# Interaction and deep network of a recommendation model: two accumulator banks used in turn, spreads in groups of three, and a new order of gathers and dumps

## What is computed

```python
emb = tables[feat_idx, sparse]                       # 2048 x 26 x 32
linear_out = lin_sparse_w[feat_idx, sparse].sum(-1) + dense @ lin_dense_w
x0 = emb; xk = emb; res = []
for w, bb in ((conv1_w, conv1_b), (conv2_w, conv2_b)):
    hp = jnp.einsum('bhd,bmd->bhmd', xk, x0).reshape(-1, h * M, E)
    xn = sigmoid(jnp.einsum('oi,bid->bod', w, hp) + bb[None, :, None])
    xk = xn[:, :half]; res.append(xn[:, half:])
cin_out = (concat(res).sum(-1) @ cin_w + cin_b)[:, 0]
h1 = tanh(deep_x @ W1 + b1); h2 = tanh(h1 @ W2 + b2); h3 = tanh(h2 @ W3 + b3)
return linear_out + cin_out + (h3 @ deep_w + deep_b)[:, 0] + bias[0]
```

## Time and profile before

| | us |
|---|---|
| median of 3 executions | 1631.12 (1628.97 to 1633.01) |
| the profiled execution, whole | 1624.22 |
| its span, first to last instruction | 1622.4 |
| PE busy | 1543.6 (95%) |
| DVE busy | 1104.7 (68%) |
| POOL busy | 709.2 (44%) |
| ACT busy | 643.5 (40%) |

### The profile page before, as it was taken

One profiled execution on the slowest core, in us unless ns is written; L12 is line 12 of the kernel. 1 busy time (PEld: TensorE's weight loads), 2 busy tenths in 40 slices (PEclk: granted clock), 3 DMA queues, 4 the chain that ended last, 5 costly groups with the idle time before them and its releaser, 6 DMA issues.

```text
span 1622.4 us, 23599 instructions
## 1 busy us (share of the span) xinstructions
PE 1543.6 (95%) x6584; PEld 656.8 (40%) x6584; DVE 1104.7 (68%) x1017; ACT 643.5 (40%) x904; POOL 709.2 (44%) x600
## 2 busy tenths in 40 slices
PE   0598999999999999999999999999999999999999
PEld 0232333333333333333333333333333336787876
DVE  3276777777777877787777777787877783333332
ACT  2342434344434443434443434434343323344443
POOL 7356565556555556565555646464731110000000
PEclk9899999999999999999999999999999999999999
DMA  6688999999999999999998989898999884634531
GB/s 126 143 183 194 231 214 223 217 231 209 226 212 225 211 224 209 221 214 229 210 228 200 232 201 231 201 240 201 237 203 235 204 210 122 186 120 147 175 104 53
DMA packets 178599, 319.80 MB, mean 197 GB/s; under 512 B 31132, under 2 KB 106812, under 8 KB 178524
## 3 DMA queue, kind: packets, MB, share of 16 engines
q1 hardware_dynamic: 155423, 298.87, 75.0%
q10 hardware_dynamic: 9828, 13.43, 4.1%
q0 software_dynamic: 13312, 7.06, 3.8%
HBM read 297.93 MB, written 21.31 MB: 197 GB/s over the span
## 4 chain that ended last, share of the span: by engine, by line
PE 86%; issue 4%; DVE 3%; another core or an unknown queue 2%; POOL 2%; DMA 1%; SPq 1%; ACT 1%; ACTq 0%; DVEq 0%; POOLq 0%
PE y L751 42%; PE xn L745 19%; PE bc L880 16%; PE bc L731 5%; PE bc L738 3%; DVE hp L692 2%; POOL emb L542 2%; PE bc L723 1%; DVE xb L692 1%; SPq L465 1%; DMA x0t<-x_halves 1%; DMA x_lo<-dense_halves 0%; ACTq L370 0%; DMA emb<-table,idx_stage 0%
## 5 line engine op out<-in xcount | busy, mean ns | idle before, releaser
L692 DVE TENSOR_TENSOR hp<-bc,xk 128x1024 f32<-128x1024 f32 x384 | 453.9, 1219 | 271.3 <-PE bc L731 136.0
L542 POOL DMA_INDIRECT emb<-table,idx_stage x416 | 515.9, 1240 | 145.5 <-issue 126.3
L692 DVE TENSOR_TENSOR xb<-xb,xk 128x1024 f32<-128x1024 f32 x448 | 546.5, 1264 | 27.9 <-ACT xk L927 23.9
L751 PE MATMUL y<-xb,w2s 128*64 128x512 f32 x1792 | 436.0, 601 | 0.0
L745 PE MATMUL xn<-sq,w1s 128*128 128x512 f32 x768 | 369.7, 618 | 4.4 <-issue 4.4
L751 PE MATMUL y<-hp,w2s 128*64 128x512 f32 x1536 | 366.0, 597 | 0.0
L553 POOL TENSOR_TENSOR r<-r 128x512 f32<-128x512 f32 x96 | 123.5, 1287 | 351.0 <-ACT r L932 181.3
L926 ACT ACTIVATE xk<-xn,bias 64x512 f32<-64x512 f32 x128 | 87.4, 683 | 438.5 <-PE xn L745 248.8
L922 ACT ACTIVATE sq<-bc 128x1024 f32<-128x1024 f32 x192 | 182.9, 1026 | 197.5 <-PE bc L738 145.8
L751 PEld LDWEIGHTS y<-xb,w2s 128*64 128x64 f32 x1792 | 116.0, 136 | 248.8 <-issue 201.5
L745 PEld LDWEIGHTS xn<-sq,w1s 128*128 128x128 f32 x768 | 137.5, 192 | 162.6 <-issue 154.8
(11 more groups left out here) (57 smaller groups left out, 843.3 us busy)
## 6 DMA issues: line engine op xcount, KB each, us to landing
xb<-x_rows SPq DMA_DIRECT2D x896, 256.0 KB
w_raw<-W SPq DMA_DIRECT2D x32, 448.0 KB
x0t<-x_halves ACTq DMA_DIRECT2D x252, 52.0 KB
x_halves<-deep_halves SPq DMA_DIRECT2D x30, 384.0 KB
w_raw<-W SPq DMA_DIRECT2D x16, 512.0 KB
emb<-table,idx_stage POOLq DMA_INDIRECT x416
x_hi<-x_halves SPq DMA_DIRECT2D x24, 256.0 KB
x_lo<-x_halves SPq DMA_DIRECT2D x24, 256.0 KB
```

What stands on the lines that cost most here:

```text
L542: nc.gpsimd.indirect_dma_start(out=emb[:, m, :], out_offset=None, in_=table, in_offset=bass.IndirectOffsetOnAxis(ap=idx_stage[:, m:m + 1], ...
L692: nc.vector.tensor_tensor(product(n)[:, :], x[:, :], xk[sl % 2][:, :], ALU.mult).then_inc(multiplied, 1)
L751: last = nc.tensor.matmul(y2[H * c:H * c + H, :], w2s[:, ORDER[n], :], src[:, c * CHUNK:(c + 1) * CHUNK], start=(n == 0), stop=(n == PAIRS ...
```

## The change

- `acc[0]` and `acc[1]` take the place of `xn` and `y2`. In step sl the first layer's half c goes to `acc[(sl + c) % 2]`, the second layer to `acc[sl % 2]`. Half 0 still waits for the reads of the last step's halves; half 1 waits for `read_y2` of the step before, which used its bank; contraction 0 waits for the read of half 0. In the prologue half 1 waits for nothing.
- PE spreads the pairs n = 3, 4, 5, 8, 9, 10 in two groups of three, with row groups 0, 1, 0 and 1, 0, 1 (`ORDER`). The order on PE is now: K fills; contractions 8 to 10; D fills; contractions 11, 12; fills 3, 4, 5; first half 0; first half 1; fills 8, 9, 10; contractions 0 to 7. All slots of a group are waited for ahead of it. DMA spreads n = 0, 1, 2, 6, 7, 11, 12.
- The last step has an order of its own (`FINAL_WORK`), and the linear terms come after all its contractions but the last five.
- The turning of the next tile's rows is in step 1 for tile 0 too. `dump_halves` and `dump` are issued together at the end of step 1's spreads.
- POOL gathers the last seven fields of a tile ahead of the sum of `r2`, not around it. In tile 0 thirteen gathers are issued at once, and thirteen one by one, each after one product of step 0 (`multiplied`).
- The 16 loads of the deep network's first group are issued in four parts in the four steps of tile 15, not all in its last step.

Changed lines of the diff (context and blank lines are left out):

```diff
@@ -52,8 +52,8 @@
-ORDER = [0, 1, 2, 3, 8, 4, 5, 9, 6, 7, 10, 11, 12]
-BY_PE = (3, 4, 6, 7, 9, 10)
+ORDER = [0, 1, 2, 3, 8, 4, 5, 6, 9, 7, 10, 11, 12]
+BY_PE = (3, 4, 5, 8, 9, 10)
@@ -65,12 +65,18 @@
-    ("fill", (3, 4)),
+    ("fill", (3, 4, 5)),
+    ("first", 1),
+    ("fill", (8, 9, 10)),
+    ("of_this", (0, 1, 2, 3, 4, 5, 6, 7)),
+)
+FINAL_WORK = (
+    ("of_last", (8, 9, 10, 11, 12)),
+    ("fill", (3, 4, 5)),
-    ("fill", (6, 7)),
-    ("first", 1),
-    ("fill", (9, 10)),
+    ("fill", (8, 9, 10)),
@@ -81,9 +87,8 @@
-def deep_step(ahead):
-    return 2 if ahead == 3 else 1
+DEEP_STEP = 1
@@ -91,7 +96,7 @@
-    if ahead == 0 or sl != deep_step(ahead):
+    if ahead == 0 or sl != DEEP_STEP:
@@ -112,7 +117,7 @@
-assert all(group_of(BY_PE[i]) != group_of(BY_PE[i + 1]) for i in range(0, len(BY_PE), 2))
+assert all(group_of(n) != group_of(n + 1) for n in BY_PE if n + 1 in BY_PE)
@@ -239,8 +244,10 @@
-        xn = pb("xn", [P, CHUNK])
-        y2 = pb("y2", [P, CHUNK])
+        acc = [pb(f"acc{i}", [P, CHUNK]) for i in range(2)]
+        terms = acc[(STEPS - 2) % 2]
@@ -322,6 +329,9 @@
+        def first_acc(sl, c):
+            return acc[(sl + c) % 2]
@@ -333,7 +343,7 @@
-            tile(0, True, 3)
+            tile(0, True, 2)
@@ -478,15 +488,13 @@
-                        if i == 2 and sl == 2 and not is_first and ahead > 0:
-                            dump_halves(t + 1)
-                    if sl == 2 and is_first:
+                    if sl == DEEP_STEP and ahead > 0:
-                    if sl == deep_step(ahead) and ahead > 0:
-                    if sl == STEPS - 1 and ahead == 0:
-                        sp.wait_ge(dense_dumped, 64)
-                        load_x(0, 0, 1)
+                    if ahead == 0:
+                        if sl == 0:
+                            sp.wait_ge(dense_dumped, 64)
+                        load_x(0, sl, STEPS)
@@ -571,40 +579,33 @@
+                    for n in range(PAIRS):
+                        pool.wait_ge(multiplied, n + 1)
+                        hold()
+                        gather((PAIRS + n,), gathered)
-                        gather(range(AHEAD[2], AHEAD[2] + 3), gathered)
+                        gather(range(AHEAD[2], M), gathered)
-                    if ahead > 0:
-                        gather(range(AHEAD[2] + 3, M), gathered)
-                if is_first:
-                    gather(range(PAIRS, M), gathered)
-                elif ahead > 1:
-                    free_emb(t + 1, filled_by(t, 1, ("D", DEEP_N - 1), ahead))
+                if ahead > 1:
+                    free_emb(t + 1, filled_by(t, DEEP_STEP, ("D", DEEP_N - 1), ahead))
-                if is_first:
-                    add_up(t, 1, r2, r2_step, y2_read, 1, sum2)
-                    free_emb(t + 1, filled_by(t, 2, ("D", DEEP_N - 1), ahead))
-                    gather(range(9), gathered)
-                else:
-                    if ahead > 1:
-                        gather(range(AHEAD[0], AHEAD[0] + 3), gathered)
-                    add_up(t, 1, r2, r2_step, y2_read, 1, sum2)
-                    if ahead > 1:
-                        gather(range(AHEAD[0] + 3, AHEAD[1]), gathered)
+                if ahead > 1:
+                    gather(range(AHEAD[0], AHEAD[0] + 3), gathered)
+                add_up(t, 1, r2, r2_step, y2_read, 1, sum2)
+                if ahead > 1:
+                    gather(range(AHEAD[0] + 3, AHEAD[1]), gathered)
-                if is_first:
-                    gather(range(9, 13), gathered)
-                elif ahead > 1:
+                if ahead > 1:
-                if is_first:
-                    gather(range(13, AHEAD[2]), gathered)
-                elif ahead > 1:
+                if ahead > 1:
@@ -690,10 +691,10 @@
-                        if n == 3 and sl == deep_step(ahead) and ahead > 0:
+                        if n == 3 and sl == DEEP_STEP and ahead > 0:
-                        if n == 5 and sl == deep_step(ahead) and ahead > 0:
+                        if n == 5 and sl == DEEP_STEP and ahead > 0:
@@ -739,16 +740,16 @@
-            def contract_k(c):
+            def contract_k(c, acc_k):
-                    last = nc.tensor.matmul(xn[:, :], w1s[:, k, :], sq[k][:, cols], start=(k == 0), stop=(k == K1 - 1))
+                    last = nc.tensor.matmul(acc_k[:, :], w1s[:, k, :], sq[k][:, cols], start=(k == 0), stop=(k == K1 - 1))
-            def contract(n):
+            def contract(n, acc_y):
-                    last = nc.tensor.matmul(y2[H * c:H * c + H, :], w2s[:, ORDER[n], :], src[:, c * CHUNK:(c + 1) * CHUNK],
+                    last = nc.tensor.matmul(acc_y[H * c:H * c + H, :], w2s[:, ORDER[n], :], src[:, c * CHUNK:(c + 1) * CHUNK],
@@ -792,15 +793,14 @@
-            contract_k(0)
-            pe.wait_ge(xn_read, 1)
-            contract_k(1)
+            for c in range(2):
+                contract_k(c, first_acc(-1, c))
-                    last = nc.tensor.matmul(xn[32 * g:32 * g + 1, 0:CHUNK], w, x[:, g * CHUNK:(g + 1) * CHUNK],
+                    last = nc.tensor.matmul(terms[32 * g:32 * g + 1, 0:CHUNK], w, x[:, g * CHUNK:(g + 1) * CHUNK],
@@ -808,7 +808,7 @@
-                        nc.tensor.matmul(xn[32 * g:32 * g + 1, c * P:(c + 1) * P], lin_sum[:, t:t + 1], idf[:, :],
+                        nc.tensor.matmul(terms[32 * g:32 * g + 1, c * P:(c + 1) * P], lin_sum[:, t:t + 1], idf[:, :],
@@ -817,44 +817,46 @@
-                    for kind, what in STEP_WORK:
+                    for kind, what in FINAL_WORK if final else STEP_WORK:
-                                if is_product(use):
+                                if not is_d(use):
-                                if not is_product(use):
+                                if is_d(use):
-                                contract(n)
-                            if final and what[-1] == PAIRS - 1:
-                                pe.wait_ge(xn_read, ALL_STEPS * 2)
-                                pe.wait_ge(end_loaded, END_LOADED)
-                                pe.wait_ge(lin_done, TILES)
-                                add_term(cwd[:, :], dense_rows, start=True)
-                                add_linear()
+                                contract(n, acc[(sl - 1) % 2])
-                            if what[0] == 0 and not start:
-                                pe.wait_ge(y2_read, s)
+                            if what[0] == 0:
+                                pe.wait_ge(xn_read, s * 2 + (2 if final else 3))
-                                contract(n)
+                                contract(n, acc[sl % 2])
-                            pe.wait_ge(xn_read, s * 2 + (2 + what))
-                            contract_k(what)
+                            if what == 0:
+                                pe.wait_ge(xn_read, s * 2 + 2)
+                            elif not start:
+                                pe.wait_ge(y2_read, s)
+                            contract_k(what, first_acc(sl, what))
+                        pe.wait_ge(y2_read, s)
+                        pe.wait_ge(end_loaded, END_LOADED)
+                        pe.wait_ge(lin_done, TILES)
+                        add_term(cwd[:, :], dense_rows, start=True)
+                        add_linear()
-                            contract(n)
+                            contract(n, acc[sl % 2])
@@ -922,6 +924,7 @@
+                xn = first_acc(sl - 1, c)
@@ -929,7 +932,7 @@
-                nc.scalar.activation(r2[:, sl, :], y2[:, :], ACT.Sigmoid, bias=bias2[:, :]).then_inc(y2_read, 1)
+                nc.scalar.activation(r2[:, sl, :], acc[sl % 2][:, :], ACT.Sigmoid, bias=bias2[:, :]).then_inc(y2_read, 1)
@@ -976,9 +979,7 @@
-                            late = is_first and sl == 2
-                            if what == int(late) and (sl < 2 or ahead > 0):
+                            if what == 0 and (sl < 2 or ahead > 0):
@@ -1024,7 +1025,7 @@
-            nc.scalar.activation(orow[rows, :], xn[rows, :], ACT.Identity, bias=bias_out[rows, :]).then_inc(row_ready, 1)
+            nc.scalar.activation(orow[rows, :], terms[rows, :], ACT.Identity, bias=bias_out[rows, :]).then_inc(row_ready, 1)
```

## The result

The changed kernel took 1646.31 us (median of 4, 1643.55 to 1648.06) against 1632.07 for the kernel before on the same chip: ratio 1.0088, 95% interval 1.0067 to 1.0109. The forecast was 1601.6. The profiled execution has a span of 1646.2 us, 23.8 more than before, at a mean granted clock of 0.993 (0.995 before). The medians differ by 14.2 us only: the profiled execution of the kernel before (1624.22) was 8 us under its median, that of the changed one (1648.06) 2 over. What follows takes the 23.8 of these two executions apart. Where a number of the kernel before has no group behind it, it is from the same views of its profile.

A forecast was written before the change was run, and what follows sets the result against it. PE blocks were taken to bound the kernel, DMA next. Terms -21.4 + 3.1 + 4 - 11.3 + 1 - 2.2 - 2.7 = -29.5 from the median 1631.1 gave 1601.6 us; range 1589 to 1623, 8 in 10.

The forecast's parts named there:

- Blocks: PE's steps: fills in threes and first-layer halves in one piece, 19.02 us for 19.36; -21.4 us over 63 steps.
- (c): Rival on PE's fills of three: third fill at full price, so threes give nothing; 1629 us, 5%.
- (d): Rival on PE's fills of three: third fill's weight load exposed, 0.18 us each; +23, 1624 us, 5%.
- D's third slot: In D steps fill 5 waits on PE for the third slot's last copy: 0.2 us x 15 tiles, +3.1.
- The waits, +4: DVE pauses in the step after D, plus the deep group's loads, reaching PE: +4 us, bounds -7 to +30.
- Gathers ahead of the sum cost nothing: POOL at a tile's start: busy 44.85 of 80 us, nobody near to waiting for the sum; no cost.
- rival (a): Dumps in one piece delay spreads 0 to 2 of the next step beyond 0.8 us of room; 1620 us, 15%.
- Half 0 is read at t + 6.6: ACT's read, t being fills 3, 4, 5's start: set by `x0t` load issues; contraction 0 due t + 6.68, no wait.
- Tile 0 and prologue, -12.5: Tile 0's idle and half-clock step go, -11.3, gathers +1; prologue's half 1 no longer waits, -2.2 us.
- +1 for gathers: In tile 0, D may wait a little for its gathers on POOL: +1 us, 0 to +4.
- End, -2.7: Earlier `x_lo` loads shorten PE's 2.80 us idle before the deep network; with the last step's -0.6, -2.7 us together.
- Rival (b): DMA becomes the bound: holes in its work make a tile about 82 us; 1662 us, 9%.

The follow-up runs named there:

- group 5: One holding chip: changed kernel with rows' dump later and gather runs of 7 (0.9853), 11 (1.0073) or dealt evenly (0.9815); kernel before with even gathers (0.9930).
- run 11: Eleven unbroken POOL gathers, not a kernel's number; tested on the run-of-7 kernel by putting its gathers ahead of the sum of `r2`: ratio 1.0073 to the kernel before.
- run-of-7 kernel: Changed kernel with gathers around the sum of `r2` again and the rows' dump behind the third spread of the step after D; ratio 0.9853 to the kernel before.
- group 4: One holding chip: changed kernel again (1.0146), core and dumps (1.0024), changed kernel with rows' dump later and gathers around the sum (0.9844); kernel before profiled once (1624.5 us).
- the core: Kernel before with only the two accumulators, fills in threes and last step's order; dumps, gathers, tile 0 and last loads as before. Ratio 1.0084.
- group 3: One chip without the hold: changed kernel again (0.9963), the core (1.0084), changed kernel with first tile as before (0.9975) or deep loads in last step (0.9956).
- best version: Changed kernel with rows' dump behind the third spread after D's step, gathers dealt evenly, deep loads all in the last step; 0.9846, 1592.46 us against 1617.36.
- core and dumps: Kernel before with the core's edits plus the halves' dumps at once behind step 1's spreads, nothing else; ratio 1.0024.
- group 1: The changed kernel as it is against the kernel before, on a holding chip; 1646.31 us against 1632.07, ratio 1.0088.

## Why the prediction was wrong

- **Blocks: right.** -21.4 over 63 steps; 19.3 over 58 measured. The threes at 0.66 to 0.67 and the drain paid once per piece are as taken, so rivals (c) and (d) fall. The row groups' rule of the Trainium skill that stood behind (d) (TensorE: Matmul & The Clock Gate, Part 3) isn't borne out here: a third fill with its load costs 0.22, as the K fills did.
- **D's third slot: +3.1 (0.2 x 15 is 3.0), measured nothing.** Steps with D are 20.09 to 20.11, the sum of their blocks.
- **The waits, +4: the step that failed.** Measured 46.8 on the chip of the result. Two things were in it. (1) At the start of a tile, 41: the "4.11 us ahead of the product at 526.05" were read as a pause of DVE, and priced by what they cost behind DVE's room. They were a hold, PE's signals coming late behind gathers: with the gathers dealt out evenly no "remote" wait is left in the kernel before past 165 us, that is, behind tile 1's first step (group 5). I priced it where it stood and didn't ask what sets its length or who else waits for PE then. So "Gathers ahead of the sum cost nothing", argued from POOL's free time, is the sentence that cost most of the 41 us: it made the run 11 long instead of 7, which was worth 34.5 of 43 in group 5. The room of `read_y2` is about the same in both orders (half 1 is due 3.4 us after the block of pairs, contraction 0 was due 3.2 after it). With a run of 7 the new order waits 8 to 12 us in the first steps and the old one 5, so the tighter order has 3 to 7 of it. In the run-of-7 kernel of group 5 they come through SP: contraction 0, which I moved 3.5 us later and priced only for the spreads' landing, falls into the hold. The kernel before with gathers ahead was tried only on a chip without the hold; its price on the other kind is open. (2) After D, 12: rival (a) was right in mechanism and mild, 0.9 us a tile here, 1.5 on the chip of group 4. On the chips without a hold it is nearly all that is left, 13 to 19 us. The mis-sized term is the landing behind the dumps: in the step shown (t = 421.66) spread 0 is issued at t + 9.9, as forecast, but pair 2 is there at t + 21.4, not 19.3, and product 5 ends at t + 26.1, not 23.9, with the fills due at t + 25.1. Moving the rows' dump behind three spreads takes these waits to 3 us or less.
- **Half 0 is read at t + 6.6, "no wait, no room": right only because of the dumps.** I took ACT's order as set by its own issues. Before, in the step after D, these issues stood behind the halves' landing. With the dumps left there the core costs 0.84% instead of gaining (group 3); I had worked out that the spreads are issued 3.5 later, and not that the old dump would go with them: the dumps' move, priced as a risk, is what the core rests on.
- **Tile 0 and prologue, -12.5 and a step gain of 1.7 (5 steps of 0.34):** -7.2 in the result. The +1 for gathers was a wait of 5.22 and a spell at the half clock: the step with D in tile 0 takes 26.8, not 20.4.
- **End, -2.7:** +3.5. The split loads freed the network (no wait, 2.80 before) and delayed the last step's spreads by as much and more. But the kernels with the loads unsplit also take 323 to 324 from the last K fill on; what else makes that 3 to 4 more than before stays open.
- **Rival (b)** fell: the spreads' transfers keep up with steps of 19.03 when the engines are full (DMA 1.01 of the time in the best version).

On chips without the hold the changed kernel gains 0.4%, not the 1.8% forecast. By profiles (1605.7 against 1614.7 of the kernel before with only its gathers moved, whose 58 steps have no wait) it is -8.1 up to K fill 4, -18.9 of blocks, +14.8 of waits, +3.2 at the end: -9. There the misses are tile 0, the dumps and the end alone.

## To carry to other kernels

A wait in the trace that no work explains is a mechanism, not noise: find out what ends it and who else it can reach before an edit takes their room, and look in the waits view for "remote", a wait that no instruction just ended. An edit on an idle engine's queue isn't free when it makes a long piece of DMA issues: deal gathers out evenly. Before pricing a tighter order by its blocks, follow each read that it needs back through the queue of the engine that does it, in the worst step. And compare on more than one chip.

## What the runs showed of the hardware

- Behind an unbroken run of indirect gathers (one per 1.25 to 1.4 us), in three of the six groups, PE's increments reach ACT, DVE and SP late: in the rows shown, ACT is released 2.8 to 3.7 us after the last issue of the run and SP 2.0 after it; ACT's idle times are up to 11.6 us long. With 11 in a row most first steps take 2.6 to 4.9 us more, with 13 PE stalled 6.9 once, with 7 in a row the first steps take up to 1.7 more (4.1 once in the core and dumps), and with 9 in the middle of a tile all 58 steps together wait 3. In the other three groups the changed kernel and its kin show none. What in the chip does it isn't shown.
- The traces of the chips that hold also lack records: of the 832 increments of the contractions 702 to 768 have one in the ten profiles there (718 in the changed kernel of group 1), and 828 or more in the ten of the other chips. That goes with the chip and not with the waits: the 702 are those of the changed order with even gathers, which hardly waits. Whether the recording itself has a part in it is open. The Trainium skill (NOTIFIC — the notification-queue block, 7.1 Overflow: three behaviours, one of which stalls the engine) says that a notification queue whose ring is full drops the new record, overwrites the oldest or stalls the producer, as it is set. No run here shows a full ring, or tests whether one has to do with the missing records or the late increments.
- The kernel before takes 1617 us in those three groups and 1628 to 1632 in the others. Its waits in the tiles explain only 7 us of that. But on the holding chip of group 5 even gathers alone take it from 1629.9 to 1618.0, so nearly all of the difference goes with the gathers; by what path the part beyond the 7 us comes isn't shown.
- Around the pauses of PE of 2.3 to 6.9 us shown above the granted clock was 0.50, the 1.2 GHz level, for 3 to 7 us, as in the 4.80 us block (2.80 at 2.4 GHz).
